# The first attention's row maxima: both heads' score products issued in one step, at places set by hand

## The reference, cut to what matters

```
qkv = (x @ qkv_w + qkv_b).reshape(Bw, Nw, 3, nh, dh)          # nh = 8 heads, dh = 8
attn = jnp.einsum('bnhd,bmhd->bhnm', q * scale, k)
bias = jnp.transpose(rpb_table[rel_idx], (2, 0, 1))
attn = jax.nn.softmax(attn + bias[None], axis=-1)
out = jnp.einsum('bhnm,bmhd->bnhd', attn, v)
```

## Time and profile before

| | |
|---|---|
| time, median of 3 runs | 2593.48 us (2576.27 to 2595.00) |
| the profiled execution's own time | 2582.66 us |
| its span in the trace | 2580.9 us |
| busy over the span: TensorE, VectorE, ScalarE, GpSimd | 90%, 71%, 55%, 16% |
| TensorE's mean granted clock | 0.901 of full speed |
| the first attention: pairs in the loop | from 370 to 1221 us |

### The profile page before, as it was taken

The page is one execution under the profiler, slowest core; times in us unless marked ns, Lnnn a source line. Parts: engine busy times, 40 slices in busy tenths (PEclk is TensorE's granted clock), DMA queues, the critical chain, the costliest instruction groups (busy, mean ns, idle before and its releaser), DMA issues.

```text
span 2580.9 us, 55201 instructions
## 1 busy us (share of the span) xinstructions
PE 2334.8 (90%) x20147; PEld 1072.7 (42%) x20178; DVE 1837.4 (71%) x4732; ACT 1422.1 (55%) x2576; POOL 424.9 (16%) x502
## 2 busy tenths in 40 slices
PE   8987679999999999999689998987799999699998
PEld 3326523333333333332544444576544444533333
DVE  4566768888888888884367776659767775366775
ACT  2116727777777777777045553327666667144443
POOL 2002200000000000000623332132100110411110
PEclk9997769999999999999589997655699999589999
DMA  3113620101101010030755552245612222734422
GB/s 96 25 31 102 219 66 26 39 26 36 29 26 39 26 38 27 26 65 6 164 148 154 158 146 61 65 116 155 239 45 67 69 93 44 160 75 100 97 61 60
DMA packets 254351, 208.23 MB, mean 81 GB/s; under 512 B 191571, under 2 KB 197892, under 8 KB 253828
## 3 DMA queue, kind: packets, MB, share of 16 engines
q1 hardware_dynamic: 240914, 176.43, 25.8%
q0 software_dynamic: 10368, 19.06, 2.6%
q10 hardware_dynamic: 2808, 9.22, 1.5%
HBM read 138.78 MB, written 65.90 MB: 79 GB/s over the span
## 4 chain that ended last, share of the span: by engine, by line
PE 75%; DVE 10%; ACT 5%; issue 4%; POOL 3%; DMA 2%; SPq 1%; DVEq 0%; ACTq 0%; POOLq 0%
PE ps L1580 11%; PE ps L1486 7%; PE ps L1551 6%; PE ps L2813 3%; PE ps L2293 3%; PE ps L2800 3%; PE ps L2309 3%; PE ps L1191 3%; PE ps L1165 3%; PE ps L2824 3%; PE ps L364 3%; PE ps L1576 3%; PE ps L376 2%; PE ps L1103 2%; PE ps L1106 1%
## 5 line engine op out<-in xcount | busy, mean ns | idle before, releaser
L1666 DVE TENSOR_REDUCE att_mpart<-ps 128x1 f32<-128x512 f32 x1024 | 633.9, 684 | 56.3 <-PE ps L1486 51.2
L1624 ACT ACTIVATE att_p<-ps 128x704 f32<-128x704 f32 x768 | 546.5, 760 | 215.5 <-PE ps L1551 208.3
L1580 PE MATMUL ps<-att_p,att_v 128*9 128x352 f32 x3072 | 301.3, 463 | 0.1
L1486 PE MATMUL ps<-att_kT,att_qT 64*128 64x512 bf16 x1024 | 281.2, 386 | 21.0 <-DMA att_qz<-qt_d 8.4
L1551 PE MATMUL ps<-att_qT,att_kT 64*128 64x352 bf16 x1536 | 251.5, 317 | 7.3 <-ACT att_p L1624 6.9
L1280 DVE TENSOR_REDUCE cau_mpart<-ps 128x1 f32<-128x512 f32 (+5 forms) x384 | 193.1, 552 | 81.1 <-PE ps L1106 67.9
L1247 ACT ACTIVATE cau_p<-ps 128x704 f32<-128x704 f32 (+6 forms) x272 | 171.6, 660 | 82.3 <-PE ps L1165 49.7
L1457 POOL DMA_DIRECT2D o_d<-att_o x128 | 64.3, 509 | 840.7 <-ACT att_o L1607 840.5
L1551 PEld LDWEIGHTS ps<-att_qT,att_kT 64*128 64x128 bf16 x1536 | 82.0, 93 | 273.5 <-issue 263.9
L2367 ACT ACTIVATE mo_g<-ps 128x768 f32<-128x768 f32 x176 | 133.2, 807 | 105.3 <-PE ps L2293 105.3
L2881 ACT ACTIVATE mo_act<-ps 128x512 f32<-128x512 f32 (+1 forms) x216 | 109.7, 559 | 145.2 <-PE ps L2800 145.1
(11 more groups left out here) (412 smaller groups left out, 3894.8 us busy)
## 6 DMA issues: line engine op xcount, KB each, us to landing
mo_gate<-wg_d SPq DMA_DIRECT2D x176, 192.0 KB, 4.1
mo_gate<-wg_d SPq DMA_DIRECT2D x64, 256.0 KB, 5.2
qt_d<-pre_qT SPq DMA_DIRECT2D x8, 1056.0 KB, 4.3
kt_d<-pre_kT SPq DMA_DIRECT2D x8, 1056.0 KB, 7.2
att_kT<-kt_d SPq DMA_DIRECT2D x32, 264.0 KB, 2.8
att_qT<-qt_d SPq DMA_DIRECT2D x32, 264.0 KB, 3.0
cqt_d<-cpr_qT SPq DMA_DIRECT2D x8, 1056.0 KB, 4.4
cau_qT<-cqt_d SPq DMA_DIRECT2D x16, 528.0 KB, 4.0
```

Of the source, the lines that this page charges most:

```text
L1486: mm = pe.matmul(ps[:, bank, :], qT[half(s), u, j * P:(j + 1) * P], kT[half(s), u, c * BANK:(c + 1) * BANK], start=True, stop=not near)
L1580: mm = pe.matmul(ps[32 * cg:32 * cg + DV, 7, 0:TH], v[:, u, i, s, :], p[:, r, s, :], start=i < 2, stop=i == FULL - 1)
L1624: e = act.activation(p[:, n % PRING, :, :], ps[:, bank:bank + 2, 0:TH], ACT.Exp)
L1666: red = dve.tensor_reduce(mpart[:, j, s, c:c + 1], ps[:, bank, :], AX.X, ALU.max)
```

## The change

In the kernel after, places of the side list are joined into steps. A step holds the same product of both heads (full, keys), or two of the tail queries' products, or both turns; one query product stays alone. Of 39 places 20 steps are made. A step first waits for the ring on behalf of all its places and then issues their products: both heads' products in succession, and the correction products of both behind them. Of the keys, the heads' small products alternate. AHEAD goes from 9 to 8 and BETWEEN (the places of the next pair's maxima ahead of the turns) from 3 to 4. One query product moves forward among the full ones.

```diff
--- before.py
+++ after.py
@@ -1324,15 +1324,34 @@
     third_last = [5 * t + 4 for t in range(3)]
 
 
-    maxes = [("full", s, j, c) for j in range(FULL) for c in range(2) for s in range(2)]
-    maxes += [("keys", s, 0, 0) for s in range(2)] + [("query", 0, 0, c) for c in range(3)]
+    full = [("full", s, j, c) for j in range(FULL) for c in range(2) for s in range(2)]
+    keys = [("keys", s, 0, 0) for s in range(2)]
+    query = [("query", 0, 0, c) for c in range(3)]
+    maxes = full[:20] + query[2:] + full[20:] + keys + query[:2]
     NM = len(maxes)
-    AHEAD, BETWEEN = 9, 3
+    AHEAD, BETWEEN = 8, 4
     side = ([("max", 1, m) for m in range(AHEAD, NM)] + [("max", 2, m) for m in range(BETWEEN)]
             + [("turn", 1, w) for w in range(QT)] + [("max", 2, m) for m in range(BETWEEN, AHEAD)])
     assert len(side) % MRING == 0
     place = [(m - AHEAD if m >= AHEAD else side.index(("max", 2, m))) % MRING for m in range(NM)]
-    cut = [len(side) * c // NU for c in range(NU + 1)]
+
+
+    def mates(x, y):
+        if "turn" in (x[0], y[0]):
+            return x[0] == y[0]
+        first, then = maxes[x[2]], maxes[y[2]]
+        return first[0] == then[0] and (then[1] == 1 or then[3] == 1 and first[0] == "query")
+
+
+    steps = []
+    for pos in range(len(side)):
+        if steps and len(steps[-1]) == 1 and mates(side[steps[-1][0]], side[pos]):
+            steps[-1].append(pos)
+        else:
+            steps.append([pos])
+    per_unit = [1, 1, 0, 1, 1, 0, 1, 1, 1] + [1, 1, 1, 1, 0, 1, 1, 1, 1] + [1, 0, 1, 0, 1, 1, 0, 1, 0]
+    assert sum(per_unit) == len(steps)
+    cut = [sum(per_unit[:c]) for c in range(NU + 1)]
 
     with ExitStack() as ctx:
         nm = Names(nc, ctx, const, stage)
@@ -1477,27 +1496,36 @@
                     pe.wait_ge(mx_red, pair * NM + n + 1)
                 apart(pe, const)
 
-            def max_scores(m, u):
-
-                kind, s, j, c = maxes[m]
-                bank = 4 + place[m]
+            def max_scores(ms, u):
+
+                kind, _, j, c = maxes[ms[0]]
+                heads = [(m, maxes[m][1], 4 + place[m]) for m in ms]
                 if kind == "full":
                     near = j == 0 and c == 1
-                    mm = pe.matmul(ps[:, bank, :], qT[half(s), u, j * P:(j + 1) * P], kT[half(s), u, c * BANK:(c + 1) * BANK],
-                                   start=True, stop=not near)
+                    for m, s, bank in heads:
+                        mm = pe.matmul(ps[:, bank, :], qT[half(s), u, j * P:(j + 1) * P], kT[half(s), u, c * BANK:(c + 1) * BANK],
+                                       start=True, stop=not near)
+                        if not near:
+                            mm.then_inc(mx_mm, 1)
                     if near:
+                        for m, s, bank in heads:
+                            for x in range(3):
+                                mm = pe.matmul(ps[:, bank, 384:512], eye[:, :], cor[:, 2 * u + s, x, 0:P], start=False, stop=x == 2)
+                            mm.then_inc(mx_mm, 1)
+                elif kind == "keys":
+                    for t in (*range(1, FULL), 0):
+                        for m, s, bank in heads:
+                            pe.matmul(ps[:, bank, t * TT:(t + 1) * TT], qT[half(s), u, t * P:(t + 1) * P], kT[half(s), u, TX:N],
+                                      start=True, stop=t > 0)
+                    for m, s, bank in heads:
                         for x in range(3):
-                            mm = pe.matmul(ps[:, bank, 384:512], eye[:, :], cor[:, 2 * u + s, x, 0:P], start=False, stop=x == 2)
-                elif kind == "keys":
-                    for t in range(FULL):
-                        out = ps[:, bank, t * TT:(t + 1) * TT]
-                        mm = pe.matmul(out, qT[half(s), u, t * P:(t + 1) * P], kT[half(s), u, TX:N], start=True, stop=t > 0)
-                        if t == 0:
-                            for x in range(3):
-                                mm = pe.matmul(out, eye[:, :], cor[:, 2 * u + s, x, P:160], start=False, stop=x == 2)
+                            mm = pe.matmul(ps[:, bank, 0:TT], eye[:, :], cor[:, 2 * u + s, x, P:160], start=False, stop=x == 2)
+                        mm.then_inc(mx_mm, 1)
                 else:
-                    mm = pe.matmul(ps[0:2 * TT, bank, 0:TH], qz[:, u, :], kT[:, u, c * TH:(c + 1) * TH], start=True, stop=True)
-                mm.then_inc(mx_mm, 1)
+                    for m, _, bank in heads:
+                        c = maxes[m][3]
+                        pe.matmul(ps[0:2 * TT, bank, 0:TH], qz[:, u, :], kT[:, u, c * TH:(c + 1) * TH], start=True, stop=True)\
+                            .then_inc(mx_mm, 1)
 
             def turn(w, u, pos):
                 u = u % 2
@@ -1510,9 +1538,9 @@
                     mm = pe.transpose(bank[:, 0:2 * TT], mz[0:2 * TT, u, FULL, :], eye[0:2 * TT, 0:2 * TT])
                 mm.then_inc(t_mm, 1)
 
-            def side_step(it, u, pos, last):
-
-                kind, ahead, n = side[pos]
+            def side_step(it, u, step, last):
+
+                kind, ahead, n = side[step[0]]
                 if last and u + ahead >= U:
                     return
                 k, slot = it * U + u, (u + ahead) % U
@@ -1520,25 +1548,33 @@
                     pe.wait_ge(loads[slot], (it + (u + ahead) // U + 1) * NL)
                 if kind == "turn" and n == 0:
                     pe.wait_ge(c_made, k + ahead + 1)
-                ring_free(pos, k, last)
+                for pos in step:
+                    ring_free(pos, k, last)
                 if kind == "max":
-                    max_scores(n, slot)
+                    max_scores([side[pos][2] for pos in step], slot)
                 else:
-                    turn(n, slot, pos)
+                    for pos in step:
+                        turn(side[pos][2], slot, pos)
 
             pe.wait_ge(loads[0], NL)
             for m in range(AHEAD):
                 if m > 0:
                     pe.wait_ge(mx_red, m)
-                max_scores(m, 0)
-            for pos in range(len(side)):
-                side_step(-1, U - 1, pos, False)
+                max_scores([m], 0)
+            for step in steps:
+                side_step(-1, U - 1, step, False)
+
+            def besides(it, u, n, last):
+                for s in range(cut[n], cut[n + 1]):
+                    side_step(it, u, steps[s], last)
 
             def scores(it, u, g, last):
 
                 t, parts = groups[g]
                 cols = slice(t * TH, (t + 1) * TH)
                 for c, (_, i) in enumerate(parts):
+                    if i is None:
+                        besides(it, u, first_unit[g] + c, last)
                     n = u * NU + first_unit[g] + c
                     pe.wait_ge(p_made, it * U * NU + n - 1 if n >= 2 else it * U * NU)
                     apart(pe, const)
@@ -1557,8 +1593,8 @@
                                 w = cor[:, 2 * u + s, x, P:160] if i is None else cor[:, 2 * u + s, x, 0:P]
                                 mm = pe.matmul(out, w, eye[:, :], start=False, stop=x == 2)
                     mm.then_inc(s_mm, 1)
-                    for pos in range(cut[first_unit[g] + c], cut[first_unit[g] + c + 1]):
-                        side_step(it, u, pos, last)
+                    if i is not None:
+                        besides(it, u, first_unit[g] + c, last)
 
             def values(it, u, g):
 
```

## The result

The changed kernel takes 2662.32 us (median of 4 runs, 2649.81 to 2666.73), the kernel before in the same comparison 2585.48 (2576.27 to 2595.00): a ratio of 1.029, with a 95% interval from 1.023 to 1.035. It is slower, as forecast (2660, range 2625 to 2700). The profiled execution took 2666.71, its span is 2664.9.

The account below looks back on a forecast made before the run. TensorE was taken to bound the kernel, tied to VectorE by the ring. A pair: 26.6 - 2.0 - 1.9 + 6.1 = 28.8 us; 68 for 31 pairs plus 3 ahead of the loop gave 2654, forecast 2660, range 2625 to 2700.

Parts of the forecast that it names:

- The price of a step to the next: In the three-bank ring, a two-bank step follows the step before by at least 1.25 us; TensorE needs 0.37.
- The waits: TensorE's added waits for VectorE and ScalarE with joined steps: together 6.1 us a pair, 5.4 at the lower price.
- corner group: Units 6 and 7: the near corner's six corrections fill part of the second step's wait, leaving 0.35 us.
- unit 20: Its maxima step waits 0.7 us because VectorE is in the chain behind the last query.
- behind the turns: Unit 23's step waits 0.7 us for VectorE's addition, priced at 0.69 us like a reduction.
- The work saved: TensorE's work in groups, queries, tails and correction products shrinks by 1.9 us a pair, bounds 1.6 to 2.1.
- The waits before: Groups of the kernel before exceed their lengths without waits by 2.0 us a pair, taken out and put in anew.
- The pair: One pair in the loop goes from 26.60 to 28.8 us, 2.2 more, over 31 pairs 68 us.
- Rival 3: TensorE's idle time lowers its clock; a quarter of the stage affected costs 3.5 us a pair: 2770, chance 0.05.
- Ahead of the loop: A whole side list runs there without units; joined steps make it a net 3 us longer.
- The halves of the array: They run independently, so two single places of different heads already take 0.61, not 0.83; otherwise 0.4 us more gain a pair.
- Rival 1: VectorE's reductions carry the pair if waits stay below 3.9 us: 71 us less, 2520, chance 0.06.

Follow-up runs that it names:

- the split wait: Changed kernel, but full maxima steps wait for each head's bank separately, same order and work: a plain pair takes 28.33 us against 28.55.
- the shorter reductions: Both kernels with VectorE's full reductions over 256, then 32, of 512 columns; the pair gains 1.19 us in the kernel before, 2.90 in the changed one.
- the two runs with 32 columns: Changed kernel and kernel before, each with VectorE's full reductions over 32 of 512 columns: a pair takes 25.65 and 25.41 us.
- the run without `apart`: Changed kernel without the `apart` line in `ring_free`; one waiting instruction still stood ahead of each step: steps still 1.25 us apart, no gain.
- The run with single places: Changed kernel with only the turns joined, places dealt, AHEAD 9, BETWEEN 3: pair 0.77 us less than the kernel before; one execution 2567.20 us.
- the spread list: Changed kernel with only `per_unit` altered, the same twenty joined steps spread so fewer stand close together: a pair takes 27.29 us.

## Why the prediction was right, step by step

- **The price of a step to the next**, 1.25 us, is exact (639.26 to 640.51). That "the first product of the step just before" decides, and not the joint wait, was shown by the split wait and by the shorter reductions. The reason given for its 0.15, a wait that is an instruction of its own, fits every row, but no run tests it.
- **The waits**: taken from the starts of one pair (634.05 to 662.60), three of 0.88 (foreseen 0.88); keys 0.75 (0.88); corner group 0.35 (0.35); unit 20, 0.61 (0.7); behind the turns 0.78 (0.7), with an addition of 0.69, as priced; small ones for ScalarE and for queued reductions 0.8 (0.8). Sum 5.9, foreseen 6.1.
- **The work saved**: 28.55 - 5.9 = 22.7, against 26.6 - 2.0 = 24.6: 1.9, as foreseen. The same count in the two runs with 32 columns gives 25.65 - 3.0 = 22.6 against 25.41 - 0.7 = 24.7, about 2.1. The keys lie at 0.30, in the middle of their bounds and not at the 0.4 taken.
- **The waits before**: that pair, too, tells what the 2.0 were. With the reductions short, 1.2 of them go. The other 0.7 or so were waits for ScalarE. The sum takes all of them out and prices ScalarE's anew, so it isn't touched.
- **The pair**: 28.55, foreseen 28.8. 31 times that difference is 8 us too much. VectorE is busy for 24.46 of it and idle for 4.1, foreseen 23.9 and 5: fewer reductions follow each other at 0.60, more stand alone at 0.69.
- **What was missed: the clock.** "The full clock throughout" was foreseen, and "if the clock falls" was one of the prediction's own signs of being wrong. It fell seven times, at 1.45 us each, 10 us. Rival 3 named that mechanism and priced it for a quarter of the stage; it came in 24 of some 900 us. The pairs with a crossing are 1.82 us longer than a plain pair, 0.78 before, seven times, 7 us that the sum left out. The fall is 1.45 of the 1.82 and only happens to stand in the same pair, 13 us behind the crossing; the crossing itself costs 0.37, as in the run without `apart`, less than before.
- **Luck in the total.** The pair foreseen too long and the clock foreseen full cancel: 66.5 us for the 31 distances, 68 foreseen. Besides, the forecast put 11 us on top because the median lay that far above the profiled execution. In this comparison the kernel before has a median of 2585.48, only 3 above it. In their place stand 12.7 us outside the changed stage in the execution that was profiled, which are no part of the change. From median to median the growth is 76.8 us, where 2660 says 66.5. The mechanism and the pair were right; that the total came within 3 us was partly chance.
- **Ahead of the loop**: 4.8 us, foreseen 3. The steps there are 1.46 apart where 1.48 was summed, but the waits for the chain and for the turns, which a list without units can't cover, weren't counted.
- **The halves of the array**: the changed kernel has no single places of different heads left to show it again. The run with single places has the order of the earlier trace rows, a maxima product at 619.78 ahead of a unit product at 619.84, and so has the kernel before with 32 columns, where that group takes 0.62 (652.06 to 652.68), the 0.61 of the sum.
- **Rival 1** needed waits below 3.9 us a pair. No kernel with joined full steps and whole reductions came there: the spread list leaves about 4.6 (27.29 less 22.7, tails not counted).

## What to carry to other kernels

A ring's depth counts in steps, not in banks: joining two products into one step in a ring of three leaves one step and a half in flight, and the engine that fills it sees the whole way to the reader and back. Before products are joined, compare that way (here 1.25 us) with the filler's own time between two steps (0.37). Where two products of different halves of the array are issued singly, see first whether they overlap anyway; here they did. What joining saves by itself was not measured apart from the placement; the placement with single places gained 0.77 us a pair.

## What the runs showed of the hardware that was not expected

TensorE's clock fell to 1.2 GHz for 3.4 us, seven times, in a stage where it is busy for 86% of a pair and never idle for longer than 0.73 us at a time behind its first pair. Each fall began as the second of two waits of 0.7 us, 2.5 us apart, ended; in the kernels with shorter waits or none it stayed at 2.4 GHz from the second pair to the end of the stage. A fall costs 1.5 us. And TensorE's product starts 0.06 us behind the reduction that it waits for where no waiting instruction stands between, 0.15 where one does.
